# ScalarE's pass over the turned h is moved behind the first logarithm and a copy

## The reference

```python
# layer 0: channel attention over the pixels of an image
aTa  = einsum('bpi,bpj->bij', v, v)            # 256 x 256 per image
h    = x + gamma * (v @ softmax(aTa)) + v      # v = group norm of x
# layer 1: per channel, on u = group norm of h, scaled to 0..1 by the image's min and max
m_k  = log(box_sum(u, k) + eps)                # k = 2, 4, 8, 16, a sum over k x k pixels
alpha = slope of m_k against log(k)            # per pixel and channel
sim  = correlation of m_k with its fitted line
x1   = u * excite(mean(alpha))                 # a gate per image and channel
out  = h + sim * sigmoid(bn(alpha)) + (1 - sim) * x1
```

## Time and profile before

| | |
|---|---|
| time, median of 3 runs | 6410.11 us (6399.6 to 6414.79) |
| time of the profiled execution | 6393.4 us |
| its span, first to last instruction | 6391.4 us |
| mean granted TensorE clock | 0.919 of full |
| half chunks of stage C | 256, in 8 turns of 32 |
| DRAM traffic | 671 MB read, 537 MB written |

### The profile page before, as it was taken

One profiled execution on the slowest core, in us unless ns is written; L12 is line 12 of the kernel. 1 busy time (PEld: TensorE's weight loads), 2 busy tenths in 40 slices (PEclk: granted clock), 3 DMA queues, 4 the chain that ended last, 5 costly groups with the idle time before them and its releaser, 6 DMA issues.

```text
span 6391.4 us, 108814 instructions
## 1 busy us (share of the span) xinstructions
PE 4960.6 (78%) x35320; PEld 4595.7 (72%) x35320; DVE 5222.9 (82%) x6293; ACT 4806.1 (75%) x5203; POOL 1806.0 (28%) x1361
## 2 busy tenths in 40 slices
PE   6969887788868887788868888788867777566632
PEld 5758887788858887688858887688857777466621
DVE  1349999799979999799979999799988889788830
ACT  0118887699959998699959998599958888688843
POOL 0012322333323333233323332233323332333311
PEclk9989999899979999899979999899989999788855
DMA  3545665588858888588858888588857777566668
GB/s 119 184 145 168 189 190 172 169 262 258 255 147 259 256 255 242 166 256 255 257 158 246 255 257 246 161 255 258 260 155 212 232 210 220 155 184 184 184 177 201
DMA packets 874514, 1344.68 MB, mean 210 GB/s; under 512 B 38704, under 2 KB 694096, under 8 KB 857936
## 3 DMA queue, kind: packets, MB, share of 16 engines
q1 hardware_dynamic: 800592, 1073.93, 47.7%
q0 software_dynamic: 73728, 268.47, 23.1%
HBM read 671.16 MB, written 536.87 MB: 189 GB/s over the span
## 4 chain that ended last, share of the span: by engine, by line
ACT 36%; PE 29%; issue 20%; DVE 9%; DMA 4%; ACTq 1%; POOL 1%; DVEq 0%; SPq 0%; POOLq 0%
PE even L545 12%; PE h_ps L526 6%; ACT logs L725 4%; ACT logs L763 4%; ACT logs L750 3%; ACT odd L725 3%; ACT logs L753 3%; PE g_ps L503 3%; ACT logs L749 3%; DMA qd<-p_scratch 2%; ACT xt L712 2%; PE odd L554 2%; ACT logs L773 2%; ACT qd L739 2%; ACT logs L779 2%
## 5 line engine op out<-in xcount | busy, mean ns | idle before, releaser
L545 PE MATMUL even<-band,t 128*128 128x128 f32 x12288 | 1863.5, 283 | 441.3 <-ACT logs L725 439.9
L545 PEld LDWEIGHTS even<-band,t 128*128 128x128 f32 x12288 | 1632.4, 198 | 493.9 <-issue 493.9
L407 POOL TENSOR_TENSOR t<-t 128x1024 f32<-128x1024 f32 (+3 forms) x800 | 1350.8, 1701 | 1189.2 <-DVE logs L1044 1054.8
L526 PE MATMUL h_ps<-mix,xt 128*128 128x256 f32 x4096 | 994.2, 386 | 189.9 <-ACT xt L712 189.2
L725 ACT ACTIVATE logs<-even,col 128x1024 f32<-128x1024 f32 x512 | 569.8, 1113 | 563.2 <-PE even L545 563.2
L526 PEld LDWEIGHTS h_ps<-mix,xt 128*128 128x128 f32 x4096 | 737.6, 190 | 320.1 <-ACT xt L712 239.9
L432 POOL DMA_DIRECT2D ut<-logs x256 | 225.0, 879 | 2574.0 <-DVE logs L1060 2494.0
L547 PE MATMUL even<-band,t 128*128 128x128 f32 x4096 | 791.9, 275 | 0.0
L503 PE MATMUL g_ps<-xa 128*128 128x257 f32 x2048 | 621.8, 385 | 23.5 <-DMA xa<-in_x_dram 23.5
L929 DVE CUSTOM_DVE_ANT_0 h_out<-h_ps,shift,mx 128x512 f32<-128x512 f32 x512 | 382.7, 747 | 307.3 <-PE h_ps L526 302.4
L563 PE MATMUL o_ps<-ident,qd 128*128 128x128 f32 x2048 | 358.5, 304 | 352.8 <-ACT o_sb L790 205.6
(11 more groups left out here) (185 smaller groups left out, 10084.7 us busy)
## 6 DMA issues: line engine op xcount, KB each, us to landing
xa<-in_x_dram SPq DMA_DIRECT2D x256, 512.0 KB, 8.6
xb<-in_x_dram SPq DMA_DIRECT2D x256, 512.0 KB, 8.6
h_scratch<-h_out SPq DMA_DIRECT2D x128, 1024.0 KB, 8.5
hr<-h_scratch SPq DMA_DIRECT2D x256, 512.0 KB, 6.8
q_scratch<-logs SPq DMA_DIRECT2D x256, 512.0 KB, 4.5
ut<-logs POOLq DMA_DIRECT2D x256, 512.0 KB, 6.4
p_scratch<-ut SPq DMA_DIRECT2D x256, 512.0 KB, 2.6
qd<-q_scratch SPq DMA_DIRECT2D x256, 512.0 KB, 8.4
```

The costliest lines, as they stand in the source:

```text
L407: ins = g.tensor_tensor(dst[:, hf, d:d + n, :], src[:, hf, d:d + n, :], src[:, hf, e:e + n, :], ALU.add)
L526: ins = t.matmul(h_ps[:, r * C:(r + 1) * C], xt[:, q % 2, jh, r, :], mix[:, jh, :], start=(jh == 0), stop=(jh == 1))
L545: ins = t.matmul(o, src[:, hf, at, :], band[:, which, :], start=True, stop=(which < 3))
```

## The change

In ScalarE's `half_chunk` the call of `offset` moves from ahead of the first logarithm to behind the first `copy_xt`, just ahead of the logarithm of box 2. Nothing else changes: the same instructions, with the same waits, are issued by every engine. The blank line is part of the diff.

```diff
                 if Ds:
                     scale_q(8 * (s - 3) + i, k, hf)
+                if Cs:
+                    log(u, hf, 0)
+                if Bs:
+                    copy_xt(nb, 2 * hf)
                 if tail:
+
                     offset(u - 1, nC if hf == 1 else nC - 1, 1 - hf)
-                if Cs:
-                    log(u, hf, 0)
-                if Bs:
-                    copy_xt(nb, 2 * hf)
                 if Cs:
                     log(u, hf, 2)
```

More of the change, by code:

```diff
@@ L799, in half_chunk @@
                     scale_q(8 * (s - 3) + i, k, hf)
-                if tail:
-                    offset(u - 1, nC if hf == 1 else nC - 1, 1 - hf)
                 if Cs:
@@ L805, in half_chunk @@
                     copy_xt(nb, 2 * hf)
+                if tail:
+                    offset(u - 1, nC if hf == 1 else nC - 1, 1 - hf)
                 if Cs:
```

## The result

The changed kernel takes 6247.53 us (median of 4 runs, 6245.06 to 6254.45), the kernel before 6406.2 us on the same chip: a ratio of 0.9753, 95% interval 0.9736 to 0.977, 159 us less. The forecast was 6244 us. The profiled execution has a span of 6243.6 us, 147.8 less than that of before.

The account below looks back on a forecast made before the run. The prediction took the TensorE-ScalarE exchange on `even`, with `offset` ahead of the first logarithm, as the bound. Turns 3 to 7, 2, 8 and 9 gave 114 + 0 + 40 + 12 = 166 us: 6244 us, range 6200 to 6320.

Parts of the forecast that it names:

- The number: Whole kernel: forecast median 6244 us, from a 166 us gain that takes the profiled execution from 6393.4 to 6227 us.
- What bounds the kernel: Turns 3 to 7: TensorE and ScalarE take turns on `even`, and `offset` delays the first logarithm; period 20.36 us.
- The first logarithm in turns 3 to 7: Without `offset` ahead of it, it would start 0.04 us after box 0 ends, 0.85 us earlier.
- Who can keep up: Turns 3 to 7: VectorE's need and the `hr` load just fit; period 19.6 us, gain 114 us, bounds 54 and 127.
- Box 1's margin: TensorE's box 1 waits for `offset`, forecast to end 0.32 us before box 1 starts.
- signs of being wrong: In the changed profile: box 1 waiting for `offset`, VectorE waiting for `hr` in turns 3 to 7, or granted clock under 1.00 there.
- The rival's price: Slower rival, box 1 waits for `offset`: at 1.4 us of lateness box 1 slips 1.1, about 6500 us; chance 0.03.
- Turn 8: No Gram rows, box 0 over early: 32 us from `offset` plus 8 from the clock, 40 us, bounds 20 and 57.
- VectorE's floor: Turn 8: `offset`'s 1.09 us is gained until VectorE's 19.30 us period stops it, 1.06 us per half chunk.
- the 8 us of returning clock: Turn 8: a shorter TensorE idle piece before box 2 returns 8 of the 25 us above full clock.
- Turn 9: Gain only where the first logarithm does not wait for box 0: 0.4 us x 30 = 12 us, bounds 0 and 21.
- Turn 2: First logarithm already starts when box 0 is over and VectorE is full; the move is worth 0.

## Why the prediction was right, and where it was not

*The number: right, with some luck.* The terms of the sum were 18 us too large together: they took the profiled execution to 6227 us, and the changed kernel's took 6245.5. The forecast of the median, 6244 for 6247.53, came nearer because the execution that was scaled up had been 16.7 us faster than its median, and the changed kernel's was only 2.0 us faster than its own.

*What bounds the kernel: right.* The two engines took turns on `even`, and `offset` stood in the loop. The chain after has no `offset` in it, and putting the logarithm first is all that it takes (the other order in the hole gives the same).

*The first logarithm in turns 3 to 7: right.* 0.85 us earlier was forecast from the end of box 0, and the undisturbed periods fell from 20.36 to 19.52, by 0.84. I had not seen the sequencer's 0.08 us in every second half chunk, and passed over one period of 21.01 in turn 3.

*Who can keep up: right in size, partly for another reason.* Forecast 19.6 and 114 us, measured 19.60 to 19.69 and 109. I took the loss from the landing time of `hr`, estimated to grow to 7.4 us. Its median did not get there (7.2 in 1900 to 2300, and 7.0 in 2000 to 2400, as before). Of the loss, 0.04 us on the mean are the sequencer's, and some 0.08 us come from a few long half chunks near the start of a turn, in which `hr`, the adding DMA or the store of p lands late. That these hang on the load of the DMAs is shown: with 5% less traffic turns 3 to 7 have 19.56. Why they come near the start of a turn was not tried.

*Box 1's margin: right as a mean, and not always kept.* It measured 0.42 us in place of 0.32, because the sum had counted `copy_xt` with its whole 0.60 us, where `offset` starts 0.48 us after it. It held in all but two half chunks. Two of the signs of being wrong thus appeared, a wait of box 1 for `offset` and waits for `hr` in turns 3 to 7, each too rare to move the forecast. The rival's price lacked the clock: it let box 1's slip enter the period whole, where 2.0 of 2.55 us did in the run with `offset` one step too late, but most half chunks lost another 1.6 us there to half clock.

*Turn 8: 34 us measured, 40 forecast.* At full clock the period is 19.28, 1.08 less, the size that was forecast, but not from VectorE's floor: ScalarE has no gap ahead of the first logarithm, and box 0 is over 1.12 us earlier. So `offset`'s whole time was gained, and ScalarE, with its one wait for box 2, still sets the period. Of the 8 us of returning clock 2 came: the granted clock stayed at 0.94, and the mean lies 0.77 us above that of full clock (20.05 - 19.28), where before it was 0.83. The idle piece before box 2 went from 3.02 to 1.93 us, and boxes 2 and 1 still ran at half clock in part, now in 20 of the 30 half chunks in place of 15, each of them costing less. The prediction cites the Trainium skill here (TensorE: Matmul & The Clock Gate, What's actually happening): the throttled state is the default one, and activity releases it. By that rule all 25 us could have come back. That did not occur by the move alone; with 8 and 10 added products it did, at a clock of 1.00 and 19.39 us. The trace thus agrees with the rule, and shows that the shorter idle piece was not enough.

*Turn 9: the term that failed.* "I take 0.4 us, 30 x 0.4 = 12 us" measured 1 us. The step behind it was that `offset`'s time is free wherever the first logarithm does not wait for box 0, with box 0 coming as before. TensorE in order of time, a half chunk of the kernel before and one of the changed kernel:

```profile
5750.75 1.12 PE L563 MATMUL o_ps<-ident,qd 128*128 128x128 f32 x4 [5.03 <-ACT o_sb L790]
5751.66 1.92 PE L554 MATMUL odd<-ident,hr 128*128 128x128 f32 x8
5753.37 3.58 PE L545 MATMUL even<-band,t 128*128 128x128 f32 x16
```

```profile
5587.54 1.12 PE L563 MATMUL o_ps<-ident,qd 128*128 128x128 f32 x4 [5.03 <-ACT o_sb L790]
5588.45 1.91 PE L554 MATMUL odd<-ident,hr 128*128 128x128 f32 x8
5590.15 3.60 PE L545 MATMUL even<-band,t 128*128 128x128 f32 x16
```

In both kernels box 0 starts 16.72 to 16.73 us after the first logarithm before it, and takes 2.02 us at full clock and up to 3.6 at half. Before, `offset` covered about the first 1.1 us of what the half clock added; after, all of it enters the period, and the logarithm waits for box 0 in 17 of 20 half chunks (5450 to 5850). The periods run from 18.86 to 20.46 us. Had box 0 kept the lengths that it had before (mean 2.84 us over the 30), the period would be, as an estimate, 16.73 + 2.84 + 0.08 = 19.65, a gain of 0.34 us and close to the forecast. But its mean rose to 3.15 us, which took 0.31 of that. Why it rose, no run isolates: the pattern of lengths repeats every 7 half chunks before and every 6 after, so the shorter period seems to shift the boxes against the clock's fall and return.

The chain of cause is shown by the products: TensorE idles for 5.0 us before the second `turn_back`, and the half clock is in it, in `turn_h` and in part of box 0; fill that piece and the half clock appears in box 2 behind the second piece; fill both and the move gives its 1.1 us.

*Turn 2:* nothing forecast, nothing measured.

## What to carry to other kernels

When two engines hand one buffer back and forth, look for what else stands in either queue between the handing over; move it into the hole in which its engine waits for the other, and check whose wait then starts at its end. A hole of 1.7 us covered a pass of 1.1. One place further the pass held box 1 up by 2.4 us, and the half chunks of turns 3 to 7 became 2.0 to 3.6 us longer. A gain on a path that runs through TensorE behind a long idle piece has to be counted with the clock it finds there.

## What the runs showed of the hardware

Idle pieces of 2.4 us (turn 5, with `offset` one step too late) and 2.6 us (turn 9, with 20 products in one piece) were often followed by boxes wholly or partly at half clock, box 2 with up to 3.65 us in place of 2.02. So were pieces of 1.9 us in turn 8 of the changed kernel, in 20 of 30 half chunks, while pieces of 1.7 us in turns 3 to 7 before the change left the granted clock at 1.00.

Products that nobody reads, put into the idle pieces, can cost time: 20 in one piece of turn 9 made the kernel before slower by 0.25%, since the idleness moved into the next piece (3.7 us), and 20 and 14 in both made it faster by 0.5%. The 34 products in one piece did no harm there: they ended so late that the second piece stayed at 1.4 us, and turn 9 had 19.88 at a clock of 1.00.

And where ScalarE waits for box 0, the wait whose value its sequencer has to compute first adds 0.08 us (0.10 in place of 0.02), and nothing when another instruction is running ahead of it.
